# Starting the expert stretches inside the routing, the first unit by row tile, with spare TensorE passes

## The reference

```python
x = x + attention(rmsnorm(x, norm1_scale), ...)
probs = softmax(xf @ router_W + router_b)          # xf = rmsnorm(x, norm2_scale), top 2 of 8
for eid in range(8):                               # at most 1280 rows for each expert
    h = gelu(xf[tok] @ W1[eid] + b1[eid]) @ W2[eid] + b2[eid]
    out = out.at[tok].add(gate * h)
x = layernorm(x_in + x + out)
# second layer: layernorm with gamma and beta, top 2 of 8, again 1280 rows for each expert
gu = xb @ w12;  g, u = split(gu);  yb = (silu(g) * u) @ w3
x = layernorm(x + scatter_add(weights * yb))
```

## Time and profile before

| | us |
|---|---|
| median of 3 runs | 1545.46 (1545.22 to 1546.62) |
| profiled execution, its own time | 1548.21 |
| its span, first to last instruction | 1546.3 |
| TensorE busy | 1461.0 (94% of the span) |
| VectorE busy | 1011.2 (65%) |
| GpSimd busy | 746.5 (48%) |
| ScalarE busy | 727.1 (47%) |

### The profile page before, as it was taken

One profiled execution on the slowest core, in us unless ns is written; L12 is line 12 of the kernel. 1 busy time (PEld: TensorE's weight loads), 2 busy tenths in 40 slices (PEclk: granted clock), 3 DMA queues, 4 the chain that ended last, 5 costly groups with the idle time before them and its releaser, 6 DMA issues. The chain is left out here.

```text
span 1546.3 us, 36023 instructions
## 1 busy us (share of the span) xinstructions
PE 1461.0 (94%) x11755; PEld 1419.0 (92%) x11755; DVE 1011.2 (65%) x2768; ACT 727.1 (47%) x1735; POOL 746.5 (48%) x749
## 2 busy tenths in 40 slices
PE   8999984999999999999949999999999999999993
PEld 7888864999999999999938999999999999999993
DVE  6999976667667667666565656565565655566455
ACT  4767653555455445545543334343433433344333
POOL 3677652566566566655523344433444334433433
PEclk9999995999999999999968999999999999999996
DMA  7122123244234243342613132413132131411117
GB/s 257 42 70 56 56 73 108 58 102 103 42 96 102 48 96 93 51 130 35 192 50 109 27 111 33 116 29 109 28 108 42 27 109 29 115 34 28 28 24 228
DMA packets 64547, 123.41 MB, mean 80 GB/s; under 512 B 14304, under 2 KB 52832, under 8 KB 61792
## 3 DMA queue, kind: packets, MB, share of 16 engines
q0 software_dynamic: 36416, 46.58, 18.4%
q1 hardware_dynamic: 28064, 76.02, 13.7%
HBM read 79.66 MB, written 42.90 MB: 79 GB/s over the span
## 5 line engine op out<-in xcount | busy, mean ns | idle before, releaser
L972 POOL DMA_INDIRECT acc<-ysb,IDX x160 | 258.8, 1617 | 132.4 <-ACT ysb L1074 66.3
L1111 DVE TENSOR_TENSOR E_hraw<-E_sg,bank 128x256 f32<-128x256 f32 x320 | 134.5, 420 | 282.7 <-ACT E_sg L1042 214.2
L965 POOL DMA_INDIRECT E_mg<-meta,IDX x160 | 151.0, 943 | 335.6 <-DVE E_gate L1095 308.4
L1166 PE MATMUL bank<-E_xT,ws 128*128 128x256 f32 x960 | 272.2, 284 | 5.1 <-DVE E_xT L1086 5.0
L1167 PE MATMUL bank<-E_xT,ws 128*128 128x256 f32 x960 | 271.5, 283 | 0.0
L1168 PE MATMUL bank<-E_xT,ws 128*128 128x256 f32 x960 | 271.3, 283 | 0.0
L1122 DVE TENSOR_TENSOR E_hT<-E_hraw,E_hT 128x256 fp32r<-128x256 f32 x640 | 259.9, 416 | 0.0
L1118 DVE CAST E_hT<-E_hraw 128x256 fp32r<-128x256 f32 x640 | 208.0, 325 | 62.1 <-ACT E_hraw L1045 40.2
L1042 ACT ACTIVATE E_sg<-bank 128x256 f32<-128x256 f32 x320 | 121.6, 384 | 256.3 <-PE bank L1168 243.4
L1166 PEld LDWEIGHTS bank<-E_xT,ws 128*128 128x128 f32 x960 | 183.0, 191 | 6.3 <-issue 5.8
L1166 PE MATMUL bank<-ws,E_hT 128*128 128x256 f32 x640 | 183.8, 287 | 0.0
(11 more groups left out here) (207 smaller groups left out, 3940.6 us busy)
## 6 DMA issues: line engine op xcount, KB each, us to landing
wraw<-in_w_ffn SPq DMA_DIRECT2D x8, 3072.0 KB, 10.7
wraw<-in_w_moe SPq DMA_DIRECT2D x8, 2048.0 KB, 13.0
X<-acc SPq DMA_DIRECT2D x16, 512.0 KB, 5.4
acc<-x SPq DMA_DIRECT2D x32, 128.0 KB, 1.7
xn<-xn SPq DMA_DIRECT2D x32, 128.0 KB, 1.7
acc<-X POOLq DMA_DIRECT2D x4, 1024.0 KB, 8.3
acc<-X SPq DMA_DIRECT2D x8, 512.0 KB, 2.7
out<-C_xo SPq DMA_DIRECT2D x8, 512.0 KB, 5.6
```

Source lines behind the costliest of these rows:

```text
L965: nc.gpsimd.indirect_dma_start(out=mg[:, j, :], out_offset=None, in_=meta_dram, in_offset=at_slots(u, j)).then_inc(s_gm, 16)
L972: nc.gpsimd.indirect_dma_start(out=acc_dram, out_offset=at_slots(u, j), in_=ysb[:, j, :], in_offset=None, compute_op=ALU.add).then_inc(s_y ...
L1111: V.tensor_tensor(hraw[:, f % RING, :], sg[:, f % RING, :], bank[f % RING][:, UW:2 * UW], ALU.mult).then_inc(s_hm, 1)
L1166: nc.tensor.matmul(out, wh, mh, start=first, stop=False)
```

## The change

What it does, part by part:

- The tiles that receive a gather, `xg` and `mg`, and the semaphores for the first unit (`first`) are now allocated once for the whole program. GpSimd issues the first unit's gathers as the last thing in the routing blocks, as soon as `IDX` is there (`R.s_idx`): the two row gathers in `routing_phase`, the two row and the two metadata gathers in `between_phase`.
- The bias tables `b1` and `b2` (32 KB and 1 MB) are loaded at the start of `routing_phase`, not at the start of E1. The table load of ScalarE for the experts' activation (`next_table`) moves to the end of the routing blocks.
- The first unit is prepared by row tile of 128: transposes into two different banks, with their own semaphores, then two scalings and two splits for each tile. In E2 VectorE normalizes the first unit's rows, where ScalarE did.
- TensorE gets `keep_busy` passes: in E1 7 at the end of the routing, 2 at the start of the experts' block, 2 after the first tile's transposes and 4 after the second's; in E2 12, 2, 4 and 5. In the attention it gets passes over zeros (`fill`): 2 after the first transposes, 3 ahead of and 3 behind `turn_weights`, 1 behind `extend_weights`.

```diff
@@ attention_phase, block.tensor
+            def fill(count):
+                for _ in range(count):
+                    nc.tensor.matmul(b_s[:, 0:KD * SW], zeros[:, 0:P], zeros[:, :], start=True, stop=True)
             turn(0)
+            fill(2)
                 if t == 0:
                     extend_weights()
+                    fill(1)
                 if t == -1:
+                    fill(3)
                     turn_weights()
+                    fill(3)
+PASSES = {"E1": (7, 2, 2, 4), "E2": (12, 2, 4, 5)}
@@ routing_phase
         def _(sp):
+            b1, b2, s_ld = bias
+            sp.dma_start(b1[:, :], io["b1"]).then_inc(s_ld, 16)
+            sp.dma_start(b2[:, :, :].rearrange("p e d -> p (e d)"), io["b2"].partition_broadcast(P)).then_inc(s_ld, 16)
             R.store(sp)
             nc.clear_and_free_semaphores(used)
+            for b in range(2):
+                pool.wait_ge(kept[f"xn{b}"], 16 * NT // 2)
+            pool.wait_ge(R.s_idx, 1)
+            gather_x(nc, io["xn1"], IDX, xg, 0, s_first)
             R.rows(act)
+            R.next_table()
             R.place(pe)
+            keep_busy(nc, bank[7], ws0, PASSES["E1"][0])
@@ expert_phase, block.gpsimd
-            x_rows(0)
-            meta_rows(0)
+            if not glu:
+                meta_rows(0)
             free_rows(1)
             x_rows(1)
@@ block.scalar
-            nc.scalar.activation(warm[:, :], cst[:, C_EPS:C_EPS + 1], ACT.Silu if glu else ACT.Gelu)
-            if glu:
-                normal_rows(1)
-            act.wait_ge(s_tg, 1)
-            raw_rows()
+            for j in range(UT):
+                act.wait_ge(s_t0 if j == 0 else s_tg, 1)
+                for k in range(KD):
+                    nc.scalar.activation(xraw[:, k, j * P:(j + 1) * P], t0_ps[j][:, k, :], ACT.Identity, scale=scb[:, k:k + 1],
+                                         bias=scb[:, KD + k:KD + k + 1]).then_inc(s_xr0 if j == 0 else s_xr, 1)
@@ block.vector
-            split_rows(1)
+            for j in range(UT if glu else 0):
+                dve.wait_ge(s_first[j], 32)
+                V.tensor_scalar(xgn[:, j, :], xg[:, j, :], mg[:, j, 4:5], mg[:, j, 5:6], ALU.mult, ALU.add).then_inc(s_xgn, 1)
+            for j in range(UT):
+                rows = slice(j * P, (j + 1) * P)
...
+                V.tensor_copy(xT[:, 0, :, rows], xraw[:, :, rows]).then_inc(s_xh0 if j == 0 else s_xh, 1)
...
+            gates(0, 0)
@@ block.tensor
-            turn_rows(1)
+            passes = PASSES["E2" if glu else "E1"]
+            keep_busy(nc, bank[7], ws[0], passes[1])
+            for j in range(UT):
+                if glu:
+                    pe.wait_ge(s_xgn, j + 1)
+                else:
+                    pe.wait_ge(s_first[j], 16)
+                for k in range(KD):
+                    ins = nc.tensor.transpose(t0_ps[j][:, k, :], xgn[:, j, k * P:(k + 1) * P], ident)
+                ins.then_inc(s_t0 if j == 0 else s_tg, 1)
+                keep_busy(nc, bank[7], ws[0], passes[2 + j])
+            pe.wait_ge(s_xl0, 1)
@@ between_phase, block.gpsimd
+            pool.wait_ge(R.s_ms, 16)
+            pool.wait_ge(R.s_idx, 1)
+            gather_x(nc, io["acc1"], IDX, xg, 0, s_first)
+            gather_meta(nc, io["meta2"], 6, IDX, mg, 0, s_first)
@@ between_phase, block.tensor
             R.place(pe)
+            keep_busy(nc, bank[7], ws0, PASSES["E2"][0])
```

More of the change, by code:

```diff
@@ L529, in _ @@
         def _(pe):
+            def fill(count):
+                for _ in range(count):
+                    nc.tensor.matmul(b_s[:, 0:KD * SW], zeros[:, 0:P], zeros[:, :], start=True, stop=True)
             pe.wait_ge(s_cst, 1)
-            for _ in range(WARM):
-                nc.tensor.matmul(b_to[:, 0:KD * SW], zeros[:, 0:P], zeros[:, :], start=True, stop=True)
+            fill(WARM)
             def add_chunk(n, c):
@@ L658, in __init__ @@
         self.meta_dram = io["meta1" if first else "meta2"]
+        self.warm = sb("warmf", [P, 1])
         self.best = sb("best", [P, 2, NT])
@@ L710, in columns, with next_table @@
                                      self.ohj[:, c, t, :].unsqueeze(2).to_broadcast(shape), ALU.mult).then_inc(self.s_col, 1)
+    def next_table(self):
+        self.nc.scalar.activation(self.warm[:, :], self.cst[:, C_EPS:C_EPS + 1], ACT.Gelu if self.first else ACT.Silu)
     def store(self, sp):
@@ L799, in select @@
                                      op0=ALU.is_equal, op1=ALU.mult))
-        V.scalar_tensor_tensor(out=self.IDX[:, 0:SC], in0=v_ps, scalar=-1.0, in1=self.free[:, :], op0=ALU.add, op1=ALU.add)
+        V.scalar_tensor_tensor(out=self.IDX[:, 0:SC], in0=v_ps, scalar=-1.0, in1=self.free[:, :], op0=ALU.add, op1=ALU.add).then_inc(self.s_idx, 1)
     def place(self, pe):
@@ L821, in place, with routing_phase @@
         nc.tensor.matmul(bank[3][:, 0:SC], self.hits[0:SC, :], self.cst[0:SC, C_ID:C_ID + SC], start=True, stop=True).then_inc(self.s_f, 1)
-def routing_phase(nc, bank, io, X, kept, LG, IDX, cst, small, wrg, fold, used):
+def routing_phase(nc, bank, io, X, kept, LG, IDX, cst, small, wrg, fold, used, ws0, xg, s_first, bias):
     with ExitStack() as ctx:
@@ L905, in expert_phase @@
         s_free = s_hm if glu else s_sg
+        b1, b2, s_ld = bias or (None, None, None)
         b_y, b_t = bank[4:6], bank[6]
+        t0_ps = [b[:, 0:D].rearrange("p (k n) -> p k n", k=KD) for b in b_y]
         t_ps = b_t[:, :].rearrange("p (k n) -> p k n", k=KD)
@@ L958, in x_rows @@
             def x_rows(u):
[L959 to L961 removed]
+                gather_x(nc, row_dram, IDX, xg, u, [s_gx] * UT)
             def meta_rows(u):
[L964 to L966 removed]
+                gather_meta(nc, meta_dram, MW, IDX, mg, u, [s_gm] * UT)
             def add_rows(u, each=False):
@@ L1088, in gates @@
             def gates(e, n):
-                dve.wait_ge(s_gm, n * (16 * UT) + 16 * UT)
+                if glu and isinstance(n, int) and n == 0:
+                    for j in range(UT):
+                        dve.wait_ge(s_first[j], 32)
+                else:
+                    dve.wait_ge(s_gm, n * (16 * UT) + (0 if glu else 16 * UT))
                 if not isinstance(n, int):
@@ L1471, in build @@
         kept = {k: ctx.enter_context(nc.semaphore(f"kept_{k}")) for k in ("xn0", "xn1", "x10", "x11", "plus")}
+        first = [[ctx.enter_context(nc.semaphore(f"first{i}{j}")) for j in range(UT)] for i in range(2)]
+        s_ld = ctx.enter_context(nc.semaphore("ld"))
+        xg, mg = sb("xg", [P, UT, D]), sb("mg", [P, UT, 6])
         ysb = sb("ysb", [P, UT, D])
```

70 lines of the change are left out of this document (38 added, 32 removed).

## The result

| | before | changed |
|---|---|---|
| median of 13 runs | 1544.76 (1542.89 to 1547.05) | 1542.06 (1540.44 to 1544.81) |
| profiled execution, its own time | 1548.21 | 1542.96 |
| its span | 1546.3 | 1541.0 |

The ratio is 0.9984, 95% interval 0.9976 to 0.9992: about 2.5 us faster (2.7 by the medians), where 11.1 were forecast. The spans of the two profiled executions differ by 5.3. The median of 1542.06 lies above the forecast range, which ended at 1539.2.

A forecast was written before the change was run, and what follows sets the result against it. It took TensorE's back-to-back products as the bound, with waits and a low clock where stretches begin. 2.0 + 2.6 + 1.9 - 0.3 + 4.9 = 11.1 us off 1545.46 gave 1534.4, range 1531.8 to 1539.2.

The forecast's parts named there:

- prologue and E1's start: Attention's prologue 2.0 us shorter through filled holes; E1's first product 2.6 us earlier through earlier gathers and preparation by tile.
- E1's clock: At E1's start, TensorE's passes raise the clock by about the first product: 1.9 us gained.
- wait for unit 1's gathers: In E1, unit 1's gathers beside the weight load: 0.3 us charged; rival of the full 2.2 us stall, chance 0.06.
- E2's start: All four gathers precede E2's barrier, so its first product comes 2.8 us earlier.
- E2's clock: At E2's start the clock is up before the first product: 2.5 us; with the start 5.3, taken as 4.9.
- products' own time: TensorE's back-to-back products in E1 and E2, a pass each 0.12 us, were taken as unchanged: nothing gained or lost.
- My last line: Signs of being wrong: clock rising 3 us or more behind the first products, or the products' own rate changing.
- the rival of a late clock: At E1's and E2's starts the clock rises late, since transposes lie between passes: 7.7 us gained, 1537.8; chance 0.17.
- the gather would pass the load: In E1, by the skill's turn-taking of queues, unit 1's gather is not delayed and the 0.3 us charge would be nothing.
- The prologue: Passes in the attention's prologue keep the clock up: 2.0 us, bounds 0 to 2.3; rival of no gain, chance 0.12.

The follow-up runs named there:

- c1: The changed kernel once more, unchanged, run beside other follow-up kernels; ratio to the kernel before 0.9986 (0.9977 to 0.9995).
- p5: The kernel before with 96 unused bytes ahead of E_xraw in E1 and 64 in E2, distance 224 bytes; ratio 0.9959, median 1538.9 us.
- p6: The changed kernel with 128 unused bytes ahead of E_xraw, distance 224 bytes; ratio to the kernel before 0.9903, median 1531.1 us.
- q2: The changed kernel without the `keep_busy` passes at the starts of E1 and E2 (all `PASSES` at 0); ratio to the kernel before 1.0002.
- w1: The changed kernel, but SyncE issues the next expert's weights only after unit 1's rows (in E2 also metadata) have landed; one run, 1548.9 us.
- q1: The changed kernel without the nine passes over zeros in the attention's prologue; ratio to the kernel before 0.9997 (0.9987 to 1.0007).
- m1: A kernel of nothing but one E2 unit's products, layers left out, at 16 pairs of addresses; 116.7 to 120.0 ns a product.
- m2: Products alone in three forms of the kernel, distance from weights to rows and h swept in 32-byte steps; times repeat every 256 bytes.
- m3: Products alone in E2's form, low halves of weights and rows moved 0 to 192 bytes from their high halves, 128 cases; floor 113.4 ns.
- p4: The kernel before with 64 unused bytes ahead of E_xraw in E1 and 32 in E2, distance 192 bytes; ratio 0.9851, 1524.0 us for 1548.1.
- b1: The changed kernel with rows 192 and h 224 bytes behind the weights; 1508.9, 1510.8, 1507.4, 1528.0, 1527.5 us, and a sixth run of 2408.7.
- b3: The kernel of b1 once more, unchanged; 1509.8, 1510.9, 1515.9, 1525.0, 1529.8 and 1530.4 us.

## Why the prediction was wrong

Point by point, from the two first traces:

| step, us | forecast | measured |
|---|---|---|
| prologue and E1's start | -4.6 | -5.5 (first product 267.59 to 262.10; `IDX` alone 2.5 of it in this pair of traces) |
| E1's clock | -1.9 | -2.5 (excess of the products that took 0.135 to 0.3 us) |
| wait for unit 1's gathers | +0.3 | +1.1 |
| E2's start | -2.8 | -2.5 (E1's last to E2's first product 71.9 to 69.5) |
| E2's clock | -2.5 (the two together taken as -4.9) | -2.2 (the same excess) |
| other stalls in E1 | none | -1.4 (rows of before, 0.2 to 0.5 each) |
| products' own time | 0 | +7.9 |

The sum is -5.1, the spans differ by 5.3. The same count over c1 gives about -3.5 where its span is 3.1 shorter than that of the kernel before: its products cost 4.7 us more (h in E2 at 117.3), and its stalls inside E1, the pause among them, 2.6.

**The step that failed** is the first one: "Nothing there is changed, so their length only moves", written of 9600 products that are three quarters of the span: it put a change of the products' own time at nothing and gave no reason. Their instructions were unchanged; their addresses weren't, and I never looked at what a tile allocated ahead of `ws0` does to the tiles behind it. It cost 7.9 us by count in the first trace of the changed kernel and 4.7 in c1. By the runs, 7.8 to 8.7 us of own gain (p5, p6) against 2.5 gives 5 to 6. That leaves 2 to 3 us by which the other terms were too high as well, within the noise of p5 and p6. My last line named this as what would prove me wrong, and no rival had it. The sum also has small slips: from 0.21 to 0.12 is 43% and not 45, and 20 passes in 4.71 us are 0.24 each and not 0.22. They move the forecast by a few tenths at most.

**The clock steps** held in mechanism and roughly in size: the level was up at the first products of both stretches and TensorE's short pause of 0.56 us in E2 did not bring it down, so the rival of a late clock is refuted. In q2 the passes gave 2.9 for 4.4. Part of the rest may go back in E1's first unit, where TensorE waits 1.19 us in c1 and not in q2, whose clock is low there; this rests on one trace of each. No step of the prediction had this wait.

**The wait for the gathers** was seen, with 8.4 us as the duration of a landing beside a load, and priced at 0.3 of at most 2.2. It was 1.11 here. The prediction set against the Trainium skill's turn-taking of queues (DMA: Bandwidth & Descriptors, section Queues, rings and completion order); the rows were right: the second gather went out at 262.17 and landed at 269.18, just behind the load, and without the load (w1) it took under 3 us. But the step from the page to "the gather would pass the load" was mine. The Trainium skill says in that section that an engine drains a whole packet, about 9 to 17 descriptors, from one queue before it turns to the next. The trace has 144 transfers for the load, 9 for each of 16 engines. If each is one descriptor, then by an estimate from the page's figure an engine's whole share of the load could be one such packet, with the gather waiting for all of it. No run here tests that.

**The prologue** gave 2.2 at the mask in the first two traces and 1.9 (q1) at `IDX`, for 2.0. Single pairs scatter by more than that, so I took all 17 traces of whole kernels. From 16 to 24 us the granted clock was 0.53 to 0.81 in the five without the passes and 1.00 in the twelve with them. `IDX` ended at 256.3 to 259.1 us in the five, 257.3 in the mean, and at 254.2 to 256.7 in the twelve, 255.3 in the mean: 2.0 us earlier.

## What to carry to other kernels

A change that allocates, frees or moves a tile changes the address of every tile behind it, and on a TensorE-bound kernel that can outweigh what the change does. Compare product counts in stretches without idle time, not only waits; and before you judge an edit, put both kernels at the same distances between stationary and moving tiles, or better, at a measured good one. Even then a product can have two times, so take several runs. A few unused bytes ahead of a tile are the cheapest knob this kernel had: 96 of them in each stretch gave 2%.

## What the runs showed of the hardware

- A 256-column float32r product at 2.4 GHz, with a weight load for each, took 113.4 to 120.0 ns by the distance between the stationary and the moving tile, with a period of 256 bytes, on a core where nothing else ran (m1, m2, m3). The trace shows it as fully busy and at clock 1.00 throughout.
- Some distances have two times, 4 ns apart at 192 and 64 bytes. Which one comes depends on more than the distance and can change from one unit to the next (113.5 and 117.8 ns in p4); b1 and b3 each gave runs near 1509 and near 1528 from the same program.
- TensorE's granted clock from 16 to 24 us was 1.00 in all twelve traces with passes in the holes of the prologue, and 0.53 to 0.81 in the five without; in the first of these TensorE had been idle for 1.63 and 1.11 us before it fell.
- GpSimd's first gather behind a wait in the routing came 0.90 and 0.80 us after `IDX`, where 0.28 us stood in the earlier trace rows.
- A gather issued 0.3 to 1.4 us behind a 2 MB weight load had landed 0.17 us behind the load, 7.0 and 7.3 us after its issue; without the load it took under 3 us (first trace of the changed kernel, c1, w1).
- TensorE's completion signals can come late and together: in c1 four of them came within 0.23 us, the first 2.7 us after the end that the profile gives its product.
